# Mixture-of-experts block results: scatter to a table by choice number and sum at the end, in place of an accumulating scatter into the output

## What is computed

```python
def _moe(x_flat, Wr, Wg, Wu, Wd):
    T = x_flat.shape[0]
    logits = x_flat @ Wr.T
    top_logits, top_idx = jax.lax.top_k(logits, TOP_K)
    probs = jax.nn.softmax(top_logits, axis=-1)
    cw = jnp.zeros((T, NUM_EXPERTS), x_flat.dtype)
    cw = cw.at[jnp.arange(T)[:, None], top_idx].add(probs)
    hg = jnp.einsum('eih,th->eti', Wg, x_flat)
    hu = jnp.einsum('eih,th->eti', Wu, x_flat)
    y = jnp.einsum('ehi,eti->eth', Wd, jax.nn.silu(hg) * hu)
    return jnp.einsum('eth,te->th', y, cw)
...
xn = _rmsnorm(x, w_ln2)
moe_out = _moe(xn.reshape(-1, hid), Wr, Wg, Wu, Wd).reshape(b, s, hid)
return residual + moe_out
```

## Time and profile before

| | us |
|---|---|
| median of 3 executions | 811.33 |
| lowest and highest | 806.05, 811.5 |
| profiled execution, its own time | 818.64 |
| span of the profiled execution | 816.8 |
| mean granted TensorE clock, as a share of full speed | 0.888 |

### The profile page before, as it was taken

One profiled execution on the slowest core, in us unless ns is written; L12 is line 12 of the kernel. 1 busy time (PEld: TensorE's weight loads), 2 busy tenths in 40 slices (PEclk: granted clock), 3 DMA queues, 4 the chain that ended last, 5 costly groups with the idle time before them and its releaser, 6 DMA issues. The chain is left out here.

```text
span 816.8 us, 10427 instructions
## 1 busy us (share of the span) xinstructions
PE 624.1 (76%) x3606; PEld 407.3 (50%) x3606; DVE 472.7 (58%) x1040; ACT 277.9 (34%) x535; POOL 276.0 (34%) x240
## 2 busy tenths in 40 slices
PE   3932578786768699985799889887778878778785
PEld 3721345564536578872355545543435444445443
DVE  6869988879686656847788687777312111111111
ACT  2375432222102123532366545444352211111111
POOL 3147467554477434557500000100510211121212
PEclk9965879998679999995599999999989998999988
DMA  6111200000012002499966444100283667667672
GB/s 184 39 39 52 61 1 1 0 1 0 26 49 65 13 1 80 118 181 220 175 76 82 63 66 54 28 2 8 76 282 128 185 188 233 212 210 236 191 240 43
DMA packets 43139, 79.84 MB, mean 98 GB/s; under 512 B 4624, under 2 KB 35408, under 8 KB 40144
## 3 DMA queue, kind: packets, MB, share of 16 engines
q1 hardware_dynamic: 39008, 74.05, 34.9%
q0 software_dynamic: 4080, 5.13, 3.3%
HBM read 63.46 MB, written 15.51 MB: 97 GB/s over the span
## 5 line engine op out<-in xcount | busy, mean ns | idle before, releaser
L1641 DVE TENSOR_REDUCE small<-bank 128x1 f32<-128x256 f32 (+3 forms) x256 | 107.6, 483 | 10.5 <-PE bank L914 9.6
L715 PE MATMUL bank<-wb,xt 128*128 128x512 f32 x184 | 97.9, 683 | 0.0
L2057 POOL DMA_INDIRECT out<-ys,xg x23 | 35.6, 1548 | 180.7 <-DVE ys L1893 129.6
L1885 DVE TENSOR_TENSOR bhm<-bsg,bank 128x512 f32<-128x512 f32 x23 | 15.8, 687 | 134.4 <-PE bank L715 134.4
L1937 POOL TENSOR_TENSOR al<-hm,ah 128x512 fp32r<-128x512 f32 (+1 forms) x28 | 40.9, 1460 | 90.7 <-ACT ah L1190 90.7
L912 PE MATMUL bank<-Ks,Qs 96*128 96x256 bf16 (+3 forms) x256 | 67.2, 330 | 5.3 <-DVE small L1641 3.7
L939 PE MATMUL bank<-Qs,Ks 99*128 99x512 bf16 (+3 forms) x256 | 60.4, 312 | 8.2 <-issue 4.6
L715 PEld LDWEIGHTS bank<-wb,xt 128*128 128x128 f32 x184 | 38.6, 220 | 42.8 <-issue 42.8
L1227 ACT ACTIVATE PTa<-bank 128x512 f32<-128x512 f32 (+1 forms) x96 | 43.9, 531 | 35.2 <-PE bank L941 27.4
L914 PE MATMUL bank<-maskb,identb 128*128 128x128 bf16 x256 | 55.6, 236 | 0.0
L1227 ACT ACTIVATE PTb<-bank 128x512 f32<-128x512 f32 (+1 forms) x96 | 44.0, 531 | 32.6 <-PE bank L941 27.7
(11 more groups left out here) (320 smaller groups left out, 1516.0 us busy)
## 6 DMA issues: line engine op xcount, KB each, us to landing
wb<-e_pack SPq DMA_DIRECT2D x23, 1536.0 KB, 6.7
pieces<-P SPq DMA_DIRECT2D x12, 512.0 KB, 10.1
Qs<-pieces SPq DMA_DIRECT2D x48, 128.0 KB, 5.4
Ks<-pieces SPq DMA_DIRECT2D x48, 128.0 KB, 6.0
stg<-w_pack SPq DMA_DIRECT2D x18, 256.0 KB, 2.7
wf<-t_pack SPq DMA_DIRECT2D x12, 256.0 KB, 2.7
sorted_rows<-blank SPq DMA_DIRECT2D x1, 2967.0 KB, 12.0
xg<-sorted_rows SPq DMA_DIRECT2D x23, 129.0 KB, 2.1
```

Of the source, the lines that this page charges most:

```text
L715: last = nc.tensor.matmul(outap, a, b_, start=start and i == 0, stop=stop and i == n - 1, **kw)
L1641: last = nc.vector.tensor_reduce(mxv[:, i, h:h + 1], banks[b][:, o:o + w], AX.X, ALU.max, negate=True)
L2057: nc.gpsimd.indirect_dma_start(out, bass.IndirectOffsetOnAxis(ap=moe["xg"][:, i % NXG, D + 1:D + 2].bitcast(U32), axis=0), moe["ys"][:, i ...
```

## The change

1. The accumulating scatter into `out` becomes a plain indirect DMA into a new DRAM table `results`. It has 16 x 128 rows for the two choices of 1024 tokens, and 23 x 128 that take the blank slots. The row number in `sorted_rows` therefore names choice and token: GpSimd rewrites that column with an offset of 1024 before it puts the second choices.
2. A scatter waits for no other scatter. `ys` has four buffers instead of two. Each of four semaphores counts the scatters of one buffer.
3. SyncE issues the weights of block i ahead of its rows, from block 4 on.
4. The two residual stores ahead of the blocks go. When all scatters have landed, eight loads of 256 KB read the table back, VectorE adds both results to `X` (eight additions of 128x512), and four stores of 256 KB write the output.
5. Every blank slot needs its own row number now: the blank rows are written by one DMA of 256 columns and one of two columns (23 x 128 pieces of 8 bytes).

```diff
@@ block.sync @@
-            sp.dma_start(sorted_rows.rearrange("(b p) d -> p b d", p=P),
-                         L1["blank"][:].unsqueeze(1).broadcast_to([P, BLOCKS, ROW])).then_inc(s_blank, 16)
+            by_block = sorted_rows.rearrange("(b p) d -> p b d", p=P)
+            sp.dma_start(by_block[:, :, 0:D], L1["blank"][:].unsqueeze(1).broadcast_to([P, BLOCKS, D])).then_inc(s_blank, 16)
+            sp.dma_start(by_block[:, :, D:ROW], L1["spare"][:]).then_inc(s_blank, 16)
...
             def block_rows(i):
                 if i >= NXG:
-                    sp.wait_ge(s_add, 16 * (i - NXG + 1))
+                    sp.wait_ge(s_res[i % NXG], 16 * (i // NXG))
...
-            for i in range(2):
+            for i in range(NWB - 1):
                 block_weights(i)
                 block_rows(i)
-            block_weights(2)
-            block_rows(2)
-            block_rows(3)
-            residual(0)
-            block_weights(3)
-            residual(1)
-            for i in range(NXG, BLOCKS):
+            block_rows(NXG - 1)
+            block_weights(NWB - 1)
+            for i in range(NWB, BLOCKS):
+                block_weights(i)
                 block_rows(i)
-                block_weights(i)
-            sp.wait_ge(s_out, 2 * 16)
-            sp.wait_ge(s_add, BLOCKS * 16)
+            for i in range(NXG):
+                sp.wait_ge(s_res[i], 16 * ((BLOCKS - 1 - i) // NXG + 1))
+            for h in range(NT // 2):
+                for j in range(2):
+                    r0 = (j * NT + 2 * h) * P
+                    sp.dma_start(moe["yt"][:, j, 2 * h:2 * h + 2, :], results[r0:r0 + 2 * P, :].rearrange("(t p) d -> p t d", p=P))\
+                        .then_inc(s_yt[h], 16)
+            for h in range(NT // 2):
+                sp.wait_ge(*summed.upto(h))
+                c, t0 = h // 2, h % 2 * 2 * P
+                sp.dma_start(out[c, t0:t0 + 2 * P, :].rearrange("(t p) d -> p t d", p=P), X[:, 2 * h:2 * h + 2, :])\
+                    .then_inc(s_out, 16)
+            sp.wait_ge(s_out, 16 * (NT // 2))
@@ block.vector @@
                     dve.wait_ge(*mm.upto(("dn", i)))
-                    if i >= 2:
-                        dve.wait_ge(s_add, 16 * (i - 1))
-                    nc.vector.tensor_scalar(moe["ys"][:, i % 2, :], banks[5 + 2 * (i % 2)][:, 0:D],
+                    if i >= NXG:
+                        dve.wait_ge(s_res[i % NXG], 16 * (i // NXG))
+                    nc.vector.tensor_scalar(moe["ys"][:, i % NXG, :], banks[5 + 2 * (i % 2)][:, 0:D],
                                             moe["xg"][:, i % NXG, D:D + 1], None, ALU.mult).then_inc(*by.tick(i))
+                elif op == "sum":
+                    h = it[1]
+                    x = X[:, 2 * h:2 * h + 2, :]
...
+                    dve.wait_ge(s_yt[h], 32)
+                    link(nc.vector.tensor_tensor(x, x, moe["yt"][:, 0, 2 * h:2 * h + 2, :], ALU.add))
+                    nc.vector.tensor_tensor(x, x, moe["yt"][:, 1, 2 * h:2 * h + 2, :], ALU.add).then_inc(*summed.tick(h))
@@ block.gpsimd @@
-                        nc.gpsimd.memset(L1["blank"][:, 0:D + 1], 0.0).then_inc(*blank_set.tick("zero"))
-                        nc.gpsimd.iota(L1["blank"][:, D + 1:D + 2].bitcast(I32), [[0, 1]], base=NT * P, channel_multiplier=1)\
+                        nc.gpsimd.memset(L1["blank"][:], 0.0).then_inc(*blank_set.tick("zero"))
+                        nc.gpsimd.memset(L1["spare"][:], 0.0).then_inc(*blank_set.tick("shares"))
+                        pool.wait_ge(*blank_set.upto("shares"))
+                        nc.gpsimd.iota(L1["spare"][:, :, 1].bitcast(I32), [[P, BLOCKS]], base=2 * NT * P, channel_multiplier=1)\
                             .then_inc(*blank_set.tick("rows"))
...
-                    pool.wait_ge(s_blank, 16)
+                    pool.wait_ge(s_blank, 32)
+                    if j == 1:
+                        pool.wait_ge(s_put[0], 16 * NT)
+                        nc.gpsimd.iota(rows[:, :, D + 1].bitcast(I32), [[P, NT]], base=NT * P, channel_multiplier=1)\
+                            .then_inc(*blank_set.tick("second"))
+                        pool.wait_ge(*blank_set.upto("second"))
...
                     pool.wait_ge(*by.upto(i))
-                    if i == 0:
-                        pool.wait_ge(s_out, 2 * 16)
-                    else:
-                        pool.wait_ge(s_add, 16 * i)
                     pool.wait_ge(s_xg[i % NXG], 16 * (i // NXG + 1))
                     nc.gpsimd.indirect_dma_start(
-                        out, bass.IndirectOffsetOnAxis(ap=moe["xg"][:, i % NXG, D + 1:D + 2].bitcast(U32), axis=0),
-                        moe["ys"][:, i % 2, :], None, bounds_check=(NT + 1) * P - 1, oob_is_err=True,
-                        compute_op=ALU.add).then_inc(s_add, 16)
+                        results, bass.IndirectOffsetOnAxis(ap=moe["xg"][:, i % NXG, D + 1:D + 2].bitcast(U32), axis=0),
+                        moe["ys"][:, i % NXG, :], None, bounds_check=(2 * NT + BLOCKS) * P - 1, oob_is_err=True).then_inc(s_res[i % NXG], 16)
```

More of the change, by code:

```diff
@@ L208, in build @@
                         ("Osb", [CH], F32), ("mtok", [TPC, 12], BF16), ("mT", [2, CH], BF16),
-                        ("route", [sum(n for _, n in ROUTE)], F32), ("blank", [ROW], F32), ("choice", [NT, 2], F32),
+                        ("route", [sum(n for _, n in ROUTE)], F32), ("blank", [D], F32), ("choice", [NT, 2], F32),
                         ("share", [2, NT], F32), ("hot", [2, NE, NT], F32), ("both", [NE * NT], F32),
@@ L217, in build @@
                         ("wrh", [256], F32R), ("wrl", [256], F32R)], x1_at)
-        pta, _ = plan([("PTa", [4, 1280], F32)], mlp_at)
-        moe, o = plan([("wb0", [EW], F32), ("wb1", [EW], F32), ("xg", [NXG, ROW], F32), ("ys", [2, D], F32)], slot_at[0])
+        pta, o = plan([("PTa", [4, 1280], F32)], mlp_at)
+        l1d, _ = plan([("spare", [BLOCKS, 2], F32)], o)
+        moe, o = plan([("wb0", [EW], F32), ("wb1", [EW], F32), ("xg", [NXG, ROW], F32)], slot_at[0])
         assert o <= slot_at[0] + 32768
@@ L229, in build @@
         moe.update(m)
+        m, _ = plan([("yt", [2, NT, D], F32), ("ys", [NXG, D], F32)], region + 82944)
+        moe.update(m)
         wb = [moe[f"wb{i}"] for i in range(NWB)]
-        L1 = {**l1, **l1a, **l1b, **l1c, **pta}
+        L1 = {**l1, **l1a, **l1b, **l1c, **l1d, **pta}
         CONSTS = 16 * (len(CONST) + 2)
@@ L251, in build @@
         pieces = nc.dram_tensor("pieces", [4, 3, 512, CH], BF16).ap()
+        results = nc.dram_tensor("results", [(2 * NT + BLOCKS) * P, D], F32).ap()
         sorted_rows = nc.dram_tensor("sorted_rows", [BLOCKS * P, ROW], F32).ap()
@@ L261, in build @@
         s_stack = [[sem(f"stack{i}_half{j}_loaded") for j in range(2)] for i in range(2)]
-        s_out = sem("residual_written")
+        s_out = sem("output_written")
         s_route = sem("routing_constants_loaded")
@@ L267, in build @@
         s_xg = [sem(f"block_rows{i}_loaded") for i in range(NXG)]
-        s_add = sem("block_added_to_output")
+        s_res = [sem(f"block_result{i}_put") for i in range(NXG)]
+        s_yt = [sem(f"results{i}_loaded") for i in range(NT // 2)]
         dve_chain = tally("dve_chain")
@@ L327, in build @@
         by = tally("block_result")
+        summed = tally("output_summed")
         units = [("ff", c) for c in range(NC)] + [("sw", c) for c in range(NC)]
@@ L535, in build @@
         ORDER.append(("dn", BLOCKS - 1))
+        ORDER += [("sum", h) for h in range(NT // 2)]
         def spare(c, i):
@@ L1890, in _ @@
                     dve.wait_ge(*mm.upto(("dn", i)))
-                    if i >= 2:
-                        dve.wait_ge(s_add, 16 * (i - 1))
-                    nc.vector.tensor_scalar(moe["ys"][:, i % 2, :], banks[5 + 2 * (i % 2)][:, 0:D],
+                    if i >= NXG:
+                        dve.wait_ge(s_res[i % NXG], 16 * (i // NXG))
+                    nc.vector.tensor_scalar(moe["ys"][:, i % NXG, :], banks[5 + 2 * (i % 2)][:, 0:D],
                                             moe["xg"][:, i % NXG, D:D + 1], None, ALU.mult).then_inc(*by.tick(i))
+                elif op == "sum":
+                    h = it[1]
+                    x = X[:, 2 * h:2 * h + 2, :]
+                    for pr in range(2):
+                        dve.wait_ge(*dproj.upto(("wout", 2 + h // 2, pr)))
+                    dve.wait_ge(s_yt[h], 32)
+                    link(nc.vector.tensor_tensor(x, x, moe["yt"][:, 0, 2 * h:2 * h + 2, :], ALU.add))
+                    nc.vector.tensor_tensor(x, x, moe["yt"][:, 1, 2 * h:2 * h + 2, :], ALU.add).then_inc(*summed.tick(h))
         @block.gpsimd
@@ L2151 @@
     r = _run(nc, [arrays], core_ids=[0])
-    return r.results[0]["out"][:NT * P].reshape(NC, CH, D)
+    return r.results[0]["out"]
```

7 lines of the change are left out of this document (1 added, 6 removed).

## The result

| | before | after |
|---|---|---|
| median, us | 811.41 (4 runs, 806.05 to 812.83) | 830.91 (4 runs, 829.45 to 833.92) |
| profiled execution, span | 818.64, 816.8 | 829.45, 827.6 |
| first to last result of VectorE, blocks 0 to 22 | 175.6 (633.21 to 808.82) | 188.0 (622.78 to 810.83) |
| of it, nine turns, blocks 2 to 20 | 17.12 each | 17.87 each |
| last result of VectorE to the end of the span | 8.0 | 16.8 |

The change makes the kernel slower: the ratio is 1.0247, 95% interval 1.0193 to 1.0301. The prediction of 818 was wrong; 830.91 lies 1.9 above the end of its range.

The account below looks back on a forecast made before the run. The prediction took a chain of waits, result, scatter, row load and products, to bound the block stage. Nine turns -6.9, the start +3.6 and the end +10.3 gave +7.0 us, 818 from a median of 811.3; range 800 to 829.

Parts of the forecast that it names:

- Weights and scatter thus always start together: Block stage: SyncE's weights and GpSimd's scatter of the same result both go about 0.8 us after that result.
- The turn: Two blocks: 0.8 to issue, 6.5 to land, 2.05 to TensorE, 7.0 of products; 16.35 us, over nine turns -6.9.
- L: Time from GpSimd's issue of the plain scatter to SyncE's next row load; taken as 6.5 us, bounds 4.9 and 7.5.
- A floor under it: Rows queue behind their block's weights, so they reach TensorE no sooner than 8.6 us after the result.
- the weights behind SyncE's wait at no cost: Next block's weights, behind SyncE's scatter wait, can go at 8.4 us, before their own condition at 9.0; costs nothing.
- The start, +3.6: Start of the block stage: block 4's weights run beside the first scatter, +2.7, and a longer stretch behind it, +0.9 us.
- The residual stores and `ys` buffers, 0: Dropping the two residual stores and adding the third and fourth result buffer were each worth 0.
- The end, 18.3: Last result to end: scatter 4.0, eight loads 8.3, additions 1.5, store 2.7, finish 1.8; 18.3 us, so +10.3.
- The early edit, 0: Blank rows written as small pieces before the attention: taken as 0, up to about 5 us if later work waits.
- The first rival: Scatter in the block stage still lands with the weights, after 7.5 us; +17.3 us, 829; chance 0.33.
- the second rival: Scatter gets away early, only the wait behind weights counts, TensorE keeps full clock; -8 us, 803; chance 0.12.
- The rivals of a gain: Block stage faster: full clock with early scatter, 803, or rows not waiting behind weights, 780; chance together 0.20.

Follow-up runs that it names:

- f1: Changed kernel with seven row buffers instead of four and rows of block i+2 issued ahead of the weights of block i; 778.18 us, ratio 0.9515.
- g1: Changed kernel, its own order, with a block's weights issued only after GpSimd has issued the scatter of the same result; 833.03 us, ratio 1.0185.
- f4: Kernel before with its scatter plain instead of accumulating, every wait and the SyncE order kept; 809.73 us, ratio 0.9874.
- e1: Changed kernel with SyncE's order from block 4 on as before, rows of a block ahead of its weights; 806.56 us, ratio 0.9959.
- e4: Changed kernel without the eight loads of the table and the eight additions at the end; 822.57 us, ratio 1.0161.
- e3: Changed kernel loading only 256 of 3072 columns of each block's weights from block 4 on; 771.85 us in one execution.
- e2: Kernel before with the weights of a block ahead of its rows from block 4 on, all else unchanged; 826.14 us, ratio 1.0207.
- f2: Changed kernel with seven row buffers, the weights of a block still ahead of its rows; 802.07 us, ratio 0.9808.
- f3: Kernel before, adds one after the other, with seven row buffers and rows two blocks ahead of the weights; 815.35 us, ratio 0.9954.

## Why the prediction was wrong

The steps, in its order:

1. **What bounds the stage:** right. A chain of waits set the pace before and after, and where the chain was cut (f1) the time fell by 4.9%.
2. **"Weights and scatter thus always start together":** right for even blocks (mostly 0.73 and 0.78 after the result), and the queue's packets show the consequence. It failed for odd blocks, whose weights stood behind SyncE's wait for the even scatter and went 3.0 to 3.4 after the result; those scatters had 2.3 to 2.6 of start and landed in 2.4. As the rows of the next even block are what TensorE waits for, this brought the turn nothing.
3. **The turn, "0.8 + 6.5 + 2.05 + 7.0 = 16.35 instead of 17.12":** this is the step that failed. Measured on average over nine turns: 0.8 + 6.95 + 2.15 + 7.99 = 17.87. L was 0.45 too short (the shorter issue brought little, since landing is set by the weights), and the last term a whole microsecond. I took the average of nine stretches of 7.8 and eight of 6.1 from the kernel before. But the two sizes went largely with the gaps: the nine long ones stood behind gaps of 2.02 to 2.82 us, seven of the eight short ones behind none or 0.66 to 1.79, and one behind 2.19. In the turn of the earlier trace rows it was 7.8 behind 2.56 and 6.1 behind 1.03. Now there is one gap of 3.9 to 4.4 a turn and the next block has none. Every stretch on the path now starts behind a long gap, at 0.50 to 0.62 of the clock, and takes 7.5 to 9.0. The nine turns went up by 6.7 instead of down by 6.9: 13.6 of the miss.
4. **"A floor under it", and the weights behind SyncE's wait at no cost:** the floor was right in kind, as g1 shows with a short scatter and rows that come no sooner than 8.9. That the wait costs nothing came out, but not for the reason given: results come in pairs, not every half turn, so the weights of block 7 went 3.4 after block 3's result; the rows behind them still landed at 657.3, ahead of the 658.96 at which TensorE came to them. What I did not work out is the kernel without that part of the change. Rows ahead of weights keep the plain scatter's gain (stage 163.4), weights ahead of rows lose it (188.0), and on the kernel before the same swap costs 15.3 (175.6 to 190.9). The price of the new order was the largest term, up to 24.7 us, and it stood in my sum only as a bound.
5. **The start, +3.6:** the first two blocks took 18.5 instead of 12.8, +5.7, for the same two reasons as in 3.
6. **The residual stores and `ys` buffers, 0:** nothing on the path needed them; dropping the scatters' order, the buffers' number and the stores is together worth at most 2.6 (f4 against e1).
7. **The end, 18.3:** measured 16.8, so +8.8 instead of +10.3. By its terms: from the result to the loads 3.3 instead of 4.0, since the scatter alone took 2.4 and not 3.2; the eight loads 9.4 instead of 8.3; the last additions 1.5 as forecast; the last store and the end 2.6 instead of 4.5 (it landed in 2.1, and the span ended 0.4 later, not 1.8). The loads were mis-sized by +1.1 and the rest by -2.6. Taking the reading back out (e4) shortens the end by 8.6.
8. **The early edit, 0:** right as far as the traces tell. On one chip the first result came at 625.9 to 627.2 with it (e1, e3, e4) and 624.5 without (e2), on another at 634.0 and 634.1 with it (f1, f2) and 635.6 and 638.3 without (f3, f4). The DMA of small pieces took SyncE 4.59 us to issue and landed 14.9 after its issue, and SyncE's next store came at 344.85 (344.35 before):

```profile
322.40 0.38 SPq L619 DMA_DIRECT2D sorted_rows<-blank  x1
322.82 4.59 SPq L620 DMA_DIRECT2D sorted_rows<-spare  x1
344.85 2.00 SPq L625 DMA_DIRECT2D pieces<-P  x3
```

```profile
sorted_rows<-spare SPq DMA_DIRECT2D x1, 23.0 KB, 14.9
```

The sum was +7.0 and the trace has +21.2: 13.6 from the turns, 2.1 from the start, -1.5 from the end. The first rival (slower, 829) came nearest; it had L too long (7.5 against 6.95) and the stretch too short (7.0 against 8.0), and the two errors partly cancelled: that it is near is partly luck. In the second rival the floor's turn adds up to 15.6 and not 15.65, which is worth 0.5 us. The rivals of a gain needed rows that don't wait behind weights and a scatter that gets away. f1 gave the first and made the second unnecessary, since no row load that TensorE is about to need waits for a fresh scatter, and there a block does take 5.82.

The rule of the Trainium skill ("DMA: Bandwidth & Descriptors", "Queues, rings and completion order"), that an engine drains a whole packet of a queue before it turns to the next, agrees with the trace in kind: no packet of q0 in 4.5 us beside weights. The same page's fit (section on the anatomy of one DMA on the gpsimd path) gives an estimate of 2.3 us for 128 KB; the trace agrees for a scatter alone (2.4), and not beside weights (7.0).

## What to carry to other kernels

Before reordering two loads on one queue, ask of each what it waits for and what waits for it: a small load that gates the tensor engine does not belong behind a large one, and a small write that gates the small load should not start at the same moment as the large one, though here mending only the second (g1) brought 0.6% that the intervals do not separate from nothing. Buffers that only hold indices tie a load to a far later write; they are cheap (here three more of 129 KB) and cut the tie, but their full worth comes only with the order on the queue changed as well (f2 against f1). When taking an average of TensorE stretches into a forecast, look first at which gap precedes each: the change may leave only one kind.

## What the runs showed of the hardware that was not expected

- Less than a microsecond decides. A 128-row scatter issued 0.05 us after a load of 1.5 MB landed in 7.0; with 1.26 us of start and older weights through, in 2.4 (g run, even blocks); with the same start but weights of 4.6 us before in flight, in 2.7 to 5.5 (g run, odd blocks); 5.9 us after a load, in 2.4.
- A gap costs a block about 2 us beyond its own length: 7.5 to 9.0 for the last part at even blocks behind 4 us of idleness, 7.8 behind 2.56, 6.1 behind 1.03; in the turn shown it was 3.6 us at 0.53 of the clock. The gap's length alone does not decide: behind 2.0 to 2.5 us both 6.1 and 7.8 occur (before, e1, f2), and in the g run one of the stretches behind 3.2 to 4.0 us, behind 3.32, kept the full clock and took 6.1.
- The part ahead of the stage, the same work in all these kernels but for the early edit, ended at 624.5 to 627.2 us on the chip of the e runs and at 634.0 to 638.3 on that of the f runs (g run: 634.7); medians of the kernel before were 809.7, 819.2 and 818.4 there. Chips differ here by 1%, as much as half of the effect under study. Why is open. The 10 us between the two profiled executions of the main comparison, 633.21 and 622.78, are of this size; which chips they ran on is not on record.
